# Who issues the loads of a mixture's token tiles, and who makes the low halves of its weights

## The reference, cut to what matters

```python
router_probs = softmax(layernorm(x2) @ gate_w)
topk_w, topk_idx = top_k(router_probs, 2)             # two experts per token
h   = silu(x_rep_sort @ w1[e]) * (x_rep_sort @ w3[e])  # rows sorted by expert, 256 -> 896
out = h @ w2[e]                                       # 896 -> 256
x2 + sum over the token's two rows of topk_w * out
```

## Time and profile before

| | |
|---|---|
| median of three executions | 469.48 us (468.16 to 470.0) |
| the profiled execution | 470.5 us, its span 468.7 us |
| PE busy / PEld busy | 430.1 us (92%) / 396.5 us (85%) |
| DVE / ACT / POOL busy | 216.8 (46%) / 228.3 (49%) / 208.5 us (44%) |
| chain that ended last, by engine | PE 69%, DVE 9%, DMA 6%, issue 5%, POOL 5%, ACT 3% |
| largest lines of the chain | L809 29%, L828 15%, out_rows DMA 5%, L847 4%, w_lo L481 2% |
| L491, adds | 35, 1560 ns each |
| L481, low halves on GpSimd | 18, 4419 ns each |
| granted clock over the span | 0.982 |

### The profile page before, as it was taken

One profiled execution on the slowest core, in us unless ns is written; L12 is line 12 of the kernel. 1 busy time (PEld: TensorE's weight loads), 2 busy tenths in 40 slices (PEclk: granted clock), 3 DMA queues, 4 the chain that ended last, 5 costly groups with the idle time before them and its releaser, 6 DMA issues.

```text
span 468.7 us, 12203 instructions
## 1 busy us (share of the span) xinstructions
PE 430.1 (92%) x3921; PEld 396.5 (85%) x3922; DVE 216.8 (46%) x582; ACT 228.3 (49%) x477; POOL 208.5 (44%) x209
## 2 busy tenths in 40 slices
PE   3889899999989999889999999799999999999970
PEld 2779788888878888779999999699999999999970
DVE  4457888768976785232332331232432333333320
ACT  3667677678765533556233641552363373323320
POOL 4424084655444551497621491473258168121211
PEclk9999999999999999999999999899999999999995
DMA  8734021271146238418452128117211212121121
GB/s 253 193 129 156 24 91 58 82 283 56 39 144 240 69 125 221 130 24 269 144 151 35 34 34 261 23 34 255 37 34 30 40 23 34 34 34 30 31 36 11
DMA packets 34523, 46.10 MB, mean 98 GB/s; under 512 B 3488, under 2 KB 29344, under 8 KB 34464
## 3 DMA queue, kind: packets, MB, share of 16 engines
q1 hardware_dynamic: 22304, 31.82, 20.3%
q0 software_dynamic: 6576, 8.82, 10.9%
q10 hardware_dynamic: 5584, 4.76, 3.6%
HBM read 32.63 MB, written 12.76 MB: 97 GB/s over the span
## 4 chain that ended last, share of the span: by engine, by line
PE 69%; DVE 9%; DMA 6%; issue 5%; POOL 5%; ACT 3%; ACTq 1%; POOLq 1%; DVEq 0%
PE bank L809 29%; PE twin L828 15%; DMA out_rows<-qf,x_all 5%; PE bank L847 4%; PE twin L662 3%; PE bank L542 3%; POOL w_lo L481 2%; PE bank L544 2%; PE bank L543 2%; PE bank L588 2%; DVE w_lo L1222 2%; DVE raw L1146 2%; PE bank L605 2%; PE twin L674 2%; PE twin L787 1%
## 5 line engine op out<-in xcount | busy, mean ns | idle before, releaser
L491 POOL DMA_INDIRECT out_rows<-qf,x_all x35 | 54.6, 1560 | 149.8 <-ACT qf L1051 143.4
L809 PE MATMUL bank<-w_hi,c_hi 128*128 (+1 forms) x280 | 106.1, 379 | 2.7 <-POOL w_lo L481 1.5
L809 PE MATMUL bank<-w_lo,c_hi 128*128 (+1 forms) x280 | 103.1, 368 | 0.0
L828 PE MATMUL twin<-w_hi,kv_halves 128*128 (+1 forms) x490 | 96.1, 288 | 3.2 <-DVE kv_halves L1328 2.4
L1322 DVE TENSOR_TENSOR x_all<-bank,x_all 128x448 f32<-128x448 f32 x70 | 43.4, 623 | 115.6 <-ACT x_all L1070 115.5
L1070 ACT ACTIVATE x_all<-bank 128x448 f32<-128x448 f32 x70 | 37.8, 543 | 93.4 <-PE bank L809 87.8
L828 PEld LDWEIGHTS twin<-w_hi,kv_halves 128*128 128x128 f32 x490 | 78.3, 190 | 4.1 <-DVE kv_halves L1328 2.7
L481 POOL TENSOR_TENSOR w_lo<-raw,w_hi x18 | 76.0, 4419 | 12.2 <-ACT w_hi L1063 12.2
L809 PE MATMUL bank<-w_hi,c_lo 128*128 (+1 forms) x280 | 80.2, 368 | 0.0
L1328 DVE TENSOR_TENSOR kv_halves<-bank,kv_halves 128x512 fp32r<-128x512 f32 x66 | 38.6, 624 | 75.2 <-ACT kv_halves L1075 75.2
L828 PE MATMUL twin<-w_lo,kv_halves 128*128 (+1 forms) x245 | 69.1, 282 | 0.0
(11 more groups left out here) (219 smaller groups left out, 708.7 us busy)
## 6 DMA issues: line engine op xcount, KB each, us to landing
raw<-in_w SPq DMA_DIRECT2D x24, 896.0 KB, 7.4
x_all<-bucket ACTq DMA_DIRECT2D x31, 129.0 KB, 2.1
raw<-in_ctxT SPq DMA_DIRECT2D x8, 256.0 KB, 3.5
out_rows<-x_all SPq DMA_DIRECT2D x8, 256.0 KB, 2.1
bucket<-pad_rows SPq DMA_DIRECT2D x13, 129.0 KB, 2.6
x_all<-in_x SPq DMA_DIRECT2D x2, 512.0 KB, 6.8
x_all<-bucket SPq DMA_DIRECT2D x6, 129.0 KB, 2.3
x_all<-in_x SPq DMA_DIRECT2D x1, 768.0 KB, 6.7
```

Source lines behind the costliest of these rows:

```text
L491: pool.indirect_dma_start(out=out, out_offset=bass.IndirectOffsetOnAxis(ap=x_in[:, v, D:D + 1].bitcast(U32), axis=0), in_=y[:, v, :], in_o ...
L809: last = nc.tensor.matmul(bank[b][:, 0:MC], stationary[:, k, :], w[:, bass.ds(at + (of + k * M + c * MC), MC)], start=(k == 0 and part == ...
L828: last = nc.tensor.matmul(bank[6][:, 0:D], stationary[:, k, :], w[:, bass.ds(at + (2 * W13 + k * D), D)], start=(k == 0 and part == 0 and ...
```

## The change

All loads of tiles from 4 on go to GpSimd's queue: those of tiles 4 and 5 leave SyncE, those from tile 6 leave ScalarE. They have semaphores of their own (`listed_loaded`). GpSimd's low halves of the next expert go to VectorE, one part behind each of its three groups of work. SyncE issues all eight paddings in one go and then the weights of expert 3.

```diff
@@ SyncE
-            for e in range(5):
+            for e in range(E):
                 pad(e)
-            for odd in range(2):
-                sp.wait_ge(scattered[odd], 32 * NPR)
-
-            sp.wait_ge(pad_stored[0], 16)
-            sp.wait_ge(y_added, 16)
-            sp.dma_start(x_in[:, 0, :], bucket[2 * P:3 * P, :]).then_inc(x_in_loaded[0], 16)
-            for e in range(5, E):
-                pad(e)
-
-            sp.wait_ge(pad_stored[1], 16 * 2)
-            sp.wait_ge(list_ready, 3)
-            at = sp.value_load(tab_row[0:1, AHEAD + 1:AHEAD + 2], min_val=0, max_val=PAD_AT)
-            sp.wait_ge(y_added, 16 * 2)
-            sp.dma_start(x_in[:, 1, :], bucket[bass.ds(at, P), :]).then_inc(x_in_loaded[1], 16)
@@ GpSimd
+            def load(t, u):
+                pool.wait_ge(y_added, 16 * (t - 3))
+                if isinstance(t, int) and t == AHEAD:
+                    at = 2 * P
+                else:
+                    at = pool.value_load(tab_row[0:1, bass.ds(t, 1)], min_val=0, max_val=PAD_AT)
+                pool.dma_start(x_in[:, u, :], bucket[bass.ds(at, P), :]).then_inc(listed_loaded[u], 16)
@@ GpSimd, mix(t, u)
-                if known(t):
-                    add(t - 1, (u - 1) % 4)
-                    return
-                first = pool.value_load(tab_first[0:1, bass.ds(t, 1)], min_val=0, max_val=1)
-                ...
-                low_halves((0,))
+                load(t + 2, (u + 2) % 4)
                 add(t - 1, (u - 1) % 4)
-                low_halves((1, 2))
@@ GpSimd, ahead of the mixture's loop
             scatter(NPR - 1)
+            for odd in range(2):
+                pool.wait_ge(scattered[odd], 32 * NPR)
+            pool.wait_ge(pad_stored[0], 16)
+            load(AHEAD, 0)
             add(1, 1)
+            pool.wait_ge(pad_stored[1], 16 * 2)
+            pool.wait_ge(list_ready, 3)
+            load(AHEAD + 1, 1)
             add(2, 2)
             pool.wait_ge(x2_stored[1], 16 * 2)
+            pool.wait_ge(list_ready, 7)
+            pool.wait_ge(pad_stored[2], 16 * (E - 2))
+            settle(pool)
             mix(AHEAD, 0)
-            pool.wait_ge(list_ready, 7)
-            settle(pool)
@@ TensorE, x_transposes
-                pe.wait_ge(x_in_loaded[u], 16 * (t // 4 + 1))
+                if early(t):
+                    pe.wait_ge(x_in_loaded[u], 16)
+                else:
+                    pe.wait_ge(listed_loaded[u], 16 * (t // 4))
@@ ScalarE: the function load and its call in mix
-                load(t + 2, (u + 2) % 4)
@@ VectorE
+            def low_halves(first, t, i):
+                if first is None:
+                    return
+                with dve.If(first):
+                    e = dve.value_load(tab_expert[0:1, bass.ds(t, 1)], min_val=1, max_val=E - 2)
+                    at = dve.snap(((e + 1) % 2) * WALL)
+                    dve.wait_ge(hi_ready, PIECES * e + (PIECES + 2 * i + 2))
+                    part = bass.ds(at + i * W13, W13)
+                    last = nc.vector.tensor_tensor(w_lo[:, part], raw[:, part], w_hi[:, part].bitcast(F32), ALU.subtract)
+                    if i == 2:
+                        last.then_inc(expert_ready, 1)
+
             def mix(t, u):
-                for c in range(2):
-                    gates(t, c)
+                first = None if known(t) else dve.value_load(tab_first[0:1, bass.ds(t, 1)], min_val=0, max_val=1)
+                gates(t, 0)
+                low_halves(first, t, 0)
+                gates(t, 1)
                 split_x(t + 1)
+                low_halves(first, t, 1)
                 low_g(t)
+                low_halves(first, t, 2)
```

More of the change, by code:

```diff
@@ L189, in build @@
         x_in_loaded = [sem(f"x_in_loaded{i}") for i in range(4)]
+        listed_loaded = [sem(f"listed_loaded{i}") for i in range(4)]
         xT_done, x_hi_ready, x_lo_ready = sem("xT_done"), sem("x_hi_ready"), sem("x_lo_ready")
@@ L478, in _ @@
                     inverse_roots_x(3)
-            def low_part(at, i):
-                return pool.tensor_tensor(w_lo[:, bass.ds(at + i * W13, W13)], raw[:, bass.ds(at + i * W13, W13)],
-                                          w_hi[:, bass.ds(at + i * W13, W13)].bitcast(F32), ALU.subtract)
+            def load(t, u):
[5 more added lines that the diff above has]
+                pool.dma_start(x_in[:, u, :], bucket[bass.ds(at, P), :]).then_inc(listed_loaded[u], 16)
             def add(t, v):
@@ L1025, in _ @@
                     evacuate_kv(i, o)
[L1028 to L1038, removed]
             def evacuate_x(t):
@@ L1122, in drain @@
                 ahead = (v + 2) % 4
-                act.wait_ge(x_in_loaded[ahead], 4 * (n + 1 - ahead) + 16)
+                act.wait_ge(listed_loaded[ahead], 4 * (n + 1 - ahead))
                 settle(act)
```

## The result

The changed kernel takes 479.0 us (median of 6 runs, 474.85 to 481.53) where the kernel before took 470.52 (6 runs, 468.16 to 471.8): ratio 1.0175 [1.0134, 1.0216]. The forecast was 470.0, the range ended at 475. The profiled execution took 477.65 us, its span 476.0, 7.3 more than before. The page's first part after: VectorE has 35.5 us more, GpSimd 47.0 us less, and PE is at 91%.

The account below looks back on a forecast made before the run. The prediction took TensorE (PE), busy 92% of the span, as the bound. Its terms, -4.9 - 1.7 + 1.2 + 0.95 + 5.0 + 0.3 - 0.3, gave +0.55, so 470.0 us against the median, range 465.5 to 475.

Parts of the forecast that it names:

- The start: GpSimd's queue at tiles 4 and 5: load 5 waits behind slow add 1; cost 5.0 us, ends 1.5 and 8.8.
- The clock: TensorE may lose its clock after idling 4 us at the start; cost 0.3 us, ends 0 and 1.8.
- Late products in five first tiles: VectorE's low halves delay products in tiles 7, 13, 17, 22, 26, TensorE 0.25 us late each; cost 1.2 us.
- Tile 5: TensorE already stands before these products, so the second one's whole delay counts; cost 0.95 us, ends 0.3 and 1.5.
- Expert 2's wait: Before tile 7, low halves on VectorE are ready before TensorE asks; gain 1.7 us, ends 1.0 and 1.74.
- Loads leave ScalarE: At 304 us ScalarE no longer waits for an add, its loop's jump stays; gain 4.9 us, ends 0 and 5.7.
- the jumps: ScalarE's shorter loop body might make its loop jumps cheaper, 0.75 us at each of two; taken as 0.3 gained.
- Hidden listed loads: In steady tiles GpSimd's loads, 3.0 us each, land before TensorE wants the rows; cost 0, thin beside weights.
- A: Faster rival: add 1 is not slowed by the weights, the start costs 1.5 us; 466.5 us, chance 0.20.
- B: Slower rival: GpSimd's queue binds at the weights, listed loads land late, clock costs 1.8; 474 us, chance 0.17.
- C: Faster rival: ScalarE's jumps cease to cost and first tiles cost VectorE nothing; 467.6 us, chance 0.10.
- D: Rival: the stall before 304 us is the jump's own, so the 4.9 stay lost; 475 us, chance 0.05.

Follow-up runs that it names:

- e8: The changed kernel plus 32 matmuls that compute nothing, before TensorE's wait for tile 5's rows: 495.83 us, no ratio, on a chip with a spread of 482 to 498.
- e10: e3 with TensorE's value load of the next tile's expert taken ahead of the g_transposes, for a loop body's first three tiles: 469.83 us, ratio 0.9956.
- e1: The kernel before with only the low halves moved to VectorE, loads staying with ScalarE and SyncE: 469.74 us, ratio 0.9996.
- e3: The changed kernel with the loads of tiles 4 and 5 back in SyncE's queue: 470.89 us, ratio 1.0005 to the kernel before.
- e9: e3 with the value loads of the last tiles' places moved behind the loops on GpSimd and ScalarE: 485.79 us, ratio 0.9896 to the kernel before.
- e11: e10 and e9's edit together: 465.96 us, ratio 0.99 to the kernel before.
- e5: The changed kernel with expert 3's weights held back until the add behind load 4 has landed: 488.63 us, ratio 1.0053 to the kernel before.
- e7: The kernel before with 33 more one-row DMAs from GpSimd, spread over the attention part and waited for at the end: 490.14 us, one run.
- e2: The kernel before with only the listed loads moved to GpSimd, the low halves staying there too: 510.81 us, ratio 1.0828.
- e6: e3 with VectorE's low halves spaced otherwise, part 0 behind split_x, parts 1 and 2 behind low_g: 468.64 us, ratio 0.9957.

## Why the prediction was wrong, step by step

- **The start, +5.0.** Right: 0.9 + 4.1 = 5.0, by the mechanism forecast. That it is right to the tenth is luck: add 1 went out at 178.3 instead of 177.0 (1.1 of it was there before the mixture) and needed 8.77 us (8.3 said), and 1.9 us instead of 0.6 passed between its landing and load 5's issue, while the load took 2.69 (4.5 with GpSimd's part said).
- **The clock, +0.3. Wrong: 2.7.** The step that failed is "most would lie under ScalarE's table loads behind tile 4, for which PE waits anyway". The value loads come behind ScalarE's evacuation of tile 4's g, and that waits for the g_transposes, which wait for the `output` that ran at half clock. The chain goes from `output` at 192.38 through the evacuation into those loads: they are moved, not overlapped (the chain above). e8 shows the whole sum. The upper end given, 1.8, was too low as well.
- **Late products in five first tiles, +1.2. Wrong: 4.9.** VectorE did what was computed: in the time of before the second product ends at 268.5 (276.63 less the tile's shift of 8.16), said was 268.5, and split_x at 268.8, said was 268.9. The step that failed is "PE wants it at 268.7: 0.25 us late". It looked at split_x, and not at the earlier reader of the second product, the g_transposes, nor at what PE's queue loses when it stands there: its value load for the next tile, which matmuls in the queue usually cover, is bare (0.43), and the next 24 matmuls come slower (+0.36). e10 takes away the 0.43 and half of the 0.36 and leaves some 0.4 a tile. The 4.9 lies inside the ends that were given (0 to 5.0), at their very top.
- **Tile 5, +0.95.** Right in the change: 0.8, and PE stood 1.0 longer (2.52 against 1.50). But without the start's stall (e1, e3) the same interval costs 2.0 and 1.9 over before, with 3.4 us of half clock in it; the clock was given no term there. The list of intervals over 8.33 also left out this one, 10.95 before, PE's standing behind ScalarE's value loads (e9 and e11 took it to 9.41 and 9.17). **Expert 2's wait, -1.7.** Right, 1.73.
- **Loads leave ScalarE, -4.9.** The stall went, by 5.6, so the size was near; the edit it was put down to was the wrong one. In e1 4.8 us of it are gone with the loads where they were. The loads' leaving gives the jumps, -0.73 at tile 26 in the change and 1.1 between e1 and e3, where -0.3 was said. (The forecast called the interval tile 17's; it ends with tile 18's transposes. It said 9.1 there and 8.42 came.)
- **Hidden listed loads, 0.** Right, no PE wait for rows after tile 5, and as thin beside weights as was said (about 1 us; 1.2 to 1.4 measured). The load's own 3.0 us was 2.4. The Trainium skill ("DMA: Bandwidth & Descriptors", Anatomy of one DMA, the path from GpSimd) fits 2.0 us plus the bytes over 436,000 a microsecond; for these 129 KB that is an estimate of 2.3 us, and the measured median agrees with it. Beside the weights it was up to 6.0, which that fit does not have.
- **Not in the sum at all:** GpSimd's DRAIN at the end, +1.5, and two tiles (12 and 22) in which ScalarE had waited 4.6 and 4.7 us for an add (-0.9 of the -1.7).

By size: 2.4 too little for the clock, 3.7 for the first tiles, 1.5 for the DRAIN, 1.1 that this execution had ahead of the mixture; against 0.7 and some 1.4 more gained than said. That makes +6.6 of the 6.8 between +0.5 and +7.3. Of the rivals, A fell with the start's price; B has its dear clock (2.7, over its 1.8) but none of its late listed loads; of C one half came, jumps that cost almost nothing, and the other, free first tiles, did not; D did not come. None had a dearer order on VectorE as its mechanism, though the prediction put 36 us of new work there and gave that term an upper end of 5.0.

## What to carry to other kernels

When work goes to a half-idle engine, list every reader of each product that it pushes back, the earliest first, and charge the waiting engine also for what its own queue then does in the open: its register loads and the restart, some 0.8 us here for a wait of 0.2. When the most loaded engine is made to stand for four microseconds, as here, charge the clock in full (2.7 us) unless the chain behind it has something that does not depend on it. And undo the parts of a change singly before crediting one of them: here one part did by itself what was put down to the other, and the other alone cost 8%.

## What the runs showed of the hardware that was not expected

- An accumulating indirect DMA of 128 rows landed in 3.8 us (median), in 8.8 beside the weight loads, and in 4.6 when those waited for it (e5). A plain load of as many rows from GpSimd: 2.4, and up to 6.0 beside weights.
- The last DRAIN of GpSimd's queue took 5.55 us with 67 DMAs issued there, 6.89 with 98, 7.06 with 100, and 8.24 in e7 with 100, of which 33 are of one row.
- In a wait of 3.92 us without a matmul TensorE's clock fell to half for 6.8 us (190.7 to 197.5), with matmuls running from 191.69 on; with idle-filling matmuls in that wait it did not (e8). Shorter waits went either way: e2 lost it for 3.4 us at one of 2.33 us and not at one of 2.29, e6 at one of 1.51, where the kernel before with 1.50 did not.
- An add that began at 277.82, during the VectorE low half of 276.88 (2.01 us), kept GpSimd for 2.53 us instead of 1.59. All five adds of the profile after that took over 1.65 us (2.46 to 2.85) began inside such a low half, and each was longer by what was left of it, less 0.1 us; adds beside VectorE's other instructions in the mixture were not longer. The Trainium skill ("SBUF — State Buffer", Who interferes with whom) has the later of the two blocked; the trace agrees in that the add is longer by 0.94, nearly the 1.07 us that the low half still had to run. As forecast it cost nothing.
